# A fused patch-embedding, attention and expert block on Trainium2: query weights masked by GpSimd in five pieces, the relative rows repeated by a single DMA, a tile of value weights per batch

## The reference

```python
h = tok_ref(x, W, b, class_token, pos_embed)       # 64 images -> 65 tokens of 128 channels
h = concat([h, txt], axis=1)                        # 64 x 193 x 128
h = h + attn_ref(layernorm(h), ...)
h = h + ffn_ref(layernorm(h), ...)

def attn_ref(x, ...):                               # 8 heads, q and k of 8 channels, v of 16
    qkv = group_norm(x @ W_qkv)
    logits = einsum('bhdi,bhdj->bhij', q, k) \
           + einsum('bhdi,dij->bhij', q, rpe_k) + einsum('bhdi,dij->bhij', k, rpe_q)
    attn = softmax(logits, axis=3)
    out = einsum('bhij,bhdj->bhdi', attn, v) + einsum('bhij,dij->bhdi', attn, rpe_v)
    return group_norm(out)

def ffn_ref(x, ...):                                # 8 experts of 512, top 2 of 8, dense
    for i in range(2):
        hid = gelu(einsum('btd,edf->ebtf', x * top_p[..., i:i+1], W1) + b1)
        out = out + einsum('ebtf,efd->btd', hid, W2) + b2_sum
```

## Time and profile before

| what | value |
|---|---|
| median of 3 runs | 3904.54 us (3902.61 to 3911.96) |
| profiled execution | 3891.26 us, span 3889.4 us |
| mean granted TensorE clock | 0.952 |
| busy: PE, DVE, ACT, POOL | 85%, 56%, 50%, 31% of the span |

### The profile page before, as it was taken

The page is one execution under the profiler, slowest core; times in us unless marked ns, Lnnn a source line. Parts: engine busy times, 40 slices in busy tenths (PEclk is TensorE's granted clock), DMA queues, the critical chain, the costliest instruction groups (busy, mean ns, idle before and its releaser), DMA issues.

```text
span 3889.4 us, 66829 instructions
## 1 busy us (share of the span) xinstructions
PE 3295.7 (85%) x22496; PEld 2686.9 (69%) x22496; DVE 2164.7 (56%) x4181; ACT 1953.9 (50%) x3603; POOL 1197.8 (31%) x1191
## 2 busy tenths in 40 slices
PE   4775788988888888988888889888888889888888
PEld 4664666777677666777776667776776667777776
DVE  6883455555555555555555555555555555555554
ACT  6882344544445544544455444444455445444455
POOL 0000133332333333333233333323333333323335
PEclk9997799999999999999999999999999999999999
DMA  8771111001111111001111111011111110011110
GB/s 187 153 144 49 23 25 24 12 16 22 24 22 24 24 24 24 7 19 24 24 22 24 24 24 20 9 22 24 22 24 24 24 24 9 19 22 24 22 22 5
DMA packets 263695, 124.72 MB, mean 32 GB/s; under 512 B 118494, under 2 KB 262174, under 8 KB 263326
## 3 DMA queue, kind: packets, MB, share of 16 engines
q1 hardware_dynamic: 261250, 118.87, 15.6%
q10 hardware_dynamic: 2416, 5.47, 0.4%
HBM read 106.03 MB, written 14.97 MB: 31 GB/s over the span
## 4 chain that ended last, share of the span: by engine, by line
issue 56%; POOL 21%; PE 10%; DVE 2%; SPq 1%; ACT 1%; POOLq 1%; DMA 0%; ACTq 0%; DVEq 0%
POOL gelu L914 20%; PE bank L432 3%; PE bank L508 1%; PE bank L473 1%; PE bank L461 1%; POOL gst L927 1%; PE bank L467 1%; SPq L392 1%; PE bank L441 1%; ACT gelu L842 1%; POOLq L913 0%; PE bank L445 0%; PE bank L442 0%; DVE gelu L623 0%; PE bank L531 0%
## 5 line engine op out<-in xcount | busy, mean ns | idle before, releaser
L914 POOL TENSOR_TENSOR gelu<-gelu 128x386 f32<-128x386 f32 x1024 | 1041.1, 1025 | 2105.8 <-ACT gelu L842 2102.2
L841 ACT ACTIVATE gelu<-bank,b_s 128x386 f32<-128x386 f32 x1024 | 595.4, 581 | 1080.9 <-DVE gelu L623 1068.5
L432 PE MATMUL bank<-gelu,w_s 128*128 128x386 f32 x2048 | 855.3, 504 | 33.6 <-POOL gelu L914 30.1
L623 DVE TENSOR_TENSOR gelu<-bank,ratio 128x386 f32<-128x386 f32 x1024 | 562.9, 555 | 475.5 <-PE bank L445 469.9
L441 PE MATMUL bank<-x_hi,w_hi 128*128 128x386 f32 x1024 | 542.9, 530 | 265.9 <-ACT gelu L841 264.6
L842 ACT ACTIVATE gelu<-gelu,b_s 128x386 f32<-128x386 f32 x1024 | 623.8, 609 | 0.0
L441 PEld LDWEIGHTS bank<-x_hi,w_hi 128*128 128x128 f32 x1024 | 196.5, 192 | 441.8 <-ACT gelu L841 353.4
L531 PE MATMUL bank<-k_f,q_bd 128*128 128x193 f32 x1600 | 405.2, 336 | 58.3 <-DVE a_bd L721 58.3
L432 PEld LDWEIGHTS bank<-gelu,w_s 128*128 128x128 f32 x2048 | 374.4, 194 | 82.3 <-POOL gelu L914 57.4
L881 ACT ACTIVATE lp<-bank,mx 128x193 f32<-128x193 f32 x800 | 292.2, 419 | 253.3 <-DVE mx L731 253.3
L731 DVE TENSOR_REDUCE mx<-bank 128x2 f32<-128x386 f32 (+1 forms) x416 | 226.4, 544 | 339.0 <-PE bank L532 336.0
(11 more groups left out here) (145 smaller groups left out, 4942.3 us busy)
## 6 DMA issues: line engine op xcount, KB each, us to landing
a_rep<-u_scratch SPq DMA_DIRECT2D x256, 200.0 KB, 4.7
xt<-in_x SPq DMA_DIRECT2D x192, 196.0 KB
q_bd<-q_f SPq DMA_DIRECT2D x512, 6.2 KB
txt_s<-in_txt SPq DMA_DIRECT2D x32, 128.0 KB, 2.1
u_scratch<-k_f SPq DMA_DIRECT2D x32, 100.0 KB, 2.2
u_scratch<-q_f SPq DMA_DIRECT2D x32, 100.0 KB, 2.2
out<-o_s SPq DMA_DIRECT2D x64, 48.5 KB
out<-o_s SPq DMA_DIRECT2D x64, 48.0 KB
```

What stands on the lines that cost most here:

```text
L432: mm(yb[:, 0:T2], w2_s[:, f, :], gelu1[:, f % RING, :], start=(f == 0), stop=(f == NF - 1)).then_inc(S["w2_done"], 1)
L623: v.tensor_tensor(gelu2[:, f % RING, :], zb[f % 2][:, 0:T2], ratio[:, :], ALU.mult).then_inc(S["z2_done"], 1)
L841: a(gelu1[:, f % RING, :], zb[f % 2][:, 0:T2], ACT.Gelu, bias=b1_s[:, f:f + 1]).then_inc(S["g_done"], 1)
L914: g.tensor_tensor(gelu1[:, f % RING, :], gelu1[:, f % RING, :], gelu2[:, f % RING, :], ALU.add).then_inc(S["hs_done"], 1)
```

## The change

It does three things. POOL now makes `q_bd`: five `tensor_tensor` multiplications of 128x640, `qs0` to `qs4`, of `q_f` (repeated over bh) by a new constant mask `mask_bh` (repeated over the columns); the 16 DMAs and the clearing of `q_bd` at the start are gone. `u_scratch` is laid out as (source, d, bh, column), so that a row of 3200 numbers is what a partition of `a_rep` needs, and a single DMA reads it back with each row repeated for eight partitions. There are two tiles `v_pad0` and `v_pad1`, and `vt1` moves to a place right behind `vt0`, ahead of the logits.

```diff
-EARLY = "txt mean1 var1 inv1 bc1 proj gmean gvar gaff".split()
+EARLY = "txt mean1 var1 inv1 bc1 proj gmean gvar gaff qs0 qs1 qs2".split()
-    "c c c c am0 c am1 c am2 c am3 vt0 hkeep log0 log1 ...
+    "c qs3 c qs4 c c am0 c am1 c am2 c am3 vt0 vt1 hkeep log0 log1 ...
-    "c pv0 c vt1 rec0 pv1 c rec1 place0 ...
+    "c pv0 c rec0 pv1 c rec1 place0 ...
-    ... w2t xin w2t w2t ot a otr a ocopy hres a"
+    ... w2t xin w2t w2t ot a otr qs0 a ocopy qs1 hres a qs2"
...
+QS = (0, 5, 10, 15, 20, OCT)
-        v_pad = sb("v_pad", [P, 2, H, 32])
+        v_pad = [sb(f"v_pad{b}", [P, 2, H, 32]) for b in range(2)]
...
                 for src, x in enumerate((k_f, q_f)):
-                    sp.dma_start(u_scratch[:, src, :, :], x[:, :]).then_inc(S["u_out"], 16)
-                for bh in range(BH):
-                    rows = slice(DK * bh, DK * bh + DK)
-                    sp.dma_start(q_bd[rows, :, bh, :], q_f[rows, :].rearrange("p (o r) -> p o r", r=8)).then_inc(S["q_spread"], 16)
+                    sp.dma_start(u_scratch[src, :, :, :].rearrange("d b i -> b d i"), x[:, :]).then_inc(S["u_out"], 16)
                 sp.wait_ge(S["u_out"], t * 32 + 32)
-                for r in range(8):
-                    sp.dma_start(a_rep[r:P - 7 + r:8, :, :], u_scratch[:, :, :, :].rearrange("b s d i -> (s d) b i")).then_inc(S["a_spread"], 16)
+                sp.dma_start(a_rep[:, :, :], u_scratch[:, :, :, :].rearrange("s d b i -> (s d) (b i)").unsqueeze(1)
+                             .broadcast_to([2 * DK, 8, BH * LP])).then_inc(S["a_spread"], 16)
...
             def copy_v(b, t):
                 act.wait_ge(S["vt"], t * 2 + b + 1)
-                if b == 1:
-                    act.wait_ge(S["pv_done"], t * 2 + 1)
+                if not is_first(t):
+                    act.wait_ge(S["pv_done"], t * 2 - 1 + b)
...
+                elif s[:2] == "qs":
+                    o0, o1 = QS[int(s[2]):int(s[2]) + 2]
+                    if s == "qs0":
+                        pool.wait_ge(S["norm"], t * 4 + 2)
+                        if not is_first(t):
+                            pool.wait_ge(S["log_ready"], t * FILLS)
+                    g.tensor_tensor(q_bd[:, o0:o1, :, :],
+                                    q_f[:, 8 * o0:8 * o1].rearrange("p (o r) -> p o r", r=8).unsqueeze(2).broadcast_to([P, o1 - o0, BH, 8]),
+                                    K["mask_bh"].unsqueeze(1).unsqueeze(3).broadcast_to([P, o1 - o0, BH, 8]), ALU.mult).then_inc(S["q_spread"], 1)
...
-            g.memset(q_bd[:, :, :, :], 0.0).then_inc(S["setup_pool"], 1)
```

More of the change, by code:

```diff
@@ L72 @@
 _at = 0
-for _n, _w in (("ident", P), ("ones", P), ("g8", P), ("g4", P), ("mask_r", 8), ("mask_q", 8), ("place", HD + HD + HD)):
+for _n, _w in (("ident", P), ("ones", P), ("g8", P), ("g4", P), ("mask_bh", BH), ("mask_r", 8), ("mask_q", 8), ("place", HD + HD + HD)):
     CO[_n] = (_at, _w)
@@ L96 @@
 FILLS = (OCT + 1) // 2
-N_QS, N_AS = 16 * BH, 16 * 8
+QS = (0, 5, 10, 15, 20, OCT)
 LOGS = 4
@@ L408, in _ @@
                 sp.wait_ge(S["h_ready"], t * 2 + 2)
-                tokens(t + 1, lambda: sp.wait_ge(S["log_ready"], t * FILLS) if t else sp.wait_ge(S["setup_pool"], 1))
+                tokens(t + 1, lambda: sp.wait_ge(S["log_ready"], t * FILLS) if t else None)
                 spread(t)
@@ L523, in attend @@
                     if i == 0:
-                        pe.wait_ge(S["q_spread"], t * N_QS + N_QS)
+                        pe.wait_ge(S["q_spread"], t * (len(QS) - 1) + len(QS) - 1)
                         pe.wait_ge(S["a_masked"], t * 4 + 4)
@@ L558, in attend @@
                                     hh = 2 * j + e
-                                    w = v_pad[0:jn, c, hh, :] if z == 0 else one_pad[0:jn, e, :]
+                                    w = v_pad[b][0:jn, c, hh, :] if z == 0 else one_pad[0:jn, e, :]
                                     m = mm(pv[b][32 * j:32 * j + 32, 256 * z:256 * z + LP], w,
@@ L719, in attend @@
                     if s == "am0":
-                        dve.wait_ge(S["a_spread"], t * N_AS + N_AS)
+                        dve.wait_ge(S["a_spread"], t * 16 + 16)
                     v.tensor_tensor(a_bd[:, o0:o1, :, :],
@@ L808, in _ @@
             v.memset(half[:, 1:2], 2.718281828459045).then_inc(z, 1)
-            v.memset(v_pad[:, :, :, :], 0.0).then_inc(z, 1)
+            v.memset(v_pad[0][:, :, :, :], 0.0); v.memset(v_pad[1][:, :, :, :], 0.0).then_inc(z, 1)
             dve.wait_ge(z, 5)
@@ L845, in copy_v @@
                 act.wait_ge(S["vt"], t * 2 + b + 1)
-                if b == 1:
-                    act.wait_ge(S["pv_done"], t * 2 + 1)
+                if not is_first(t):
+                    act.wait_ge(S["pv_done"], t * 2 - 1 + b)
                 for c, (j0, jn) in enumerate(JC):
-                    blk = v_pad[0:jn, c, :, :].rearrange("p h n -> p (h n)")
+                    blk = v_pad[b][0:jn, c, :, :].rearrange("p h n -> p (h n)")
                     dst = bass.AP(tensor=blk.tensor, offset=blk.offset, ap=[list(blk.ap[0]), [64, H // 2], [32 + HD, 2], [1, HD]])
@@ L948, in build @@
     tok_scratch = nc.dram_tensor("tok_scratch", (P, B, NPATCH), F32, kind="Internal").ap()
-    u_scratch = nc.dram_tensor("u_scratch", (BH, 2, DK, LP), F32, kind="Internal").ap()
+    u_scratch = nc.dram_tensor("u_scratch", (2, DK, BH, LP), F32, kind="Internal").ap()
     with ExitStack() as ctx:
@@ L968, in shape_constants @@
     put("g4", (p[:, None] // 4 == p[None] // 4) / 4.0)
+    put("mask_bh", p[:, None] // DK == np.arange(BH)[None])
     put("mask_r", p[:, None] // HD == np.arange(8)[None])
```

## The result

The changed kernel takes 3681.1 us (median; 3674.57 to 3684.06), the kernel before 3903.57 in the same comparison. The ratio is 0.9428 (95% interval 0.9403 to 0.9453): 5.7% faster, some 223 us. The prediction had the direction but said 3789, and its range ended at 3715, above the result. The profiled execution has a span of 3682.3 us.

The account below looks back on a forecast made before the run. Bound: DVE idles 6.75 us before am0 for a_rep, whose reads queue behind 16 DMAs. 31 x (1.7 + 1.7) = 105 us plus 11 in the first turn: 3891 - 116 = 3775 profiled, 3789 us median; range 3715 to 3880.

Parts of the forecast that it names:

- Part 3: Second transposes ahead of the logits: 1.70 us of PE between pv0 and pv1 go; new wait for ACT's copies before the first logit.
- The gain of the stage is 1.7 us a turn: Masking stage up to the first logit: it comes at 2109.2 instead of 2110.87, 1.7 us earlier each turn.
- walk: Forecast schedule of one turn: POOL's pieces at 1.66 us and sums, then DVE's masks alternating with sums, to the first logit.
- The end of sum 3: POOL's line of pieces and sums: sum 3 ends at 2100.9, with pieces at 1.66 us.
- The end of `am3`: DVE's last mask, alternating with POOL's sums for the port: ends at 2108.9, or 2106.9 without the exclusion.
- The first logit: PE's first logit, 1.9 us behind chunk 9 after ACT's copies and transposes: taken at 2109.2, where it was 2110.87.
- cost nothing that I can see: Slow matmuls at clock 0.55 in the 6.41 us behind the stall: no cost, since DVE is busy 6.26 us of it.
- 116: Total gain in us: 31 x (1.7 + 1.7) = 105, plus 11 in the first turn.
- `pv1`: PE between pv0 and pv1: the two transposes and the wait for copies go, 1.7 us a turn.
- Cheap pieces: Rival: POOL's pieces cost 1.0 us each, sum 3 ends at 2098.4, 5.9 us gained a turn, 3724 median; chance 0.12.
- POOL wins the port: Rival: am0 gets in only when POOL runs dry after sum 6, 0.7 us left a turn, 3872; chance 0.10.
- Dear pieces: Rival: POOL's pieces cost 3.3 us, 85 us slower, 3989; gains used up at 2.7 us a piece; chance 0.15.

Follow-up runs that it names:

- e6: Kernel before with one edit: SP issues the eight reads of a_rep ahead of the 16 DMAs into q_bd; 3660 us, 0.9329 of before.
- e3: Changed kernel, but a_rep read back by eight DMAs from the old scratch layout; 0.9422 of before.
- e1: Kernel before with only the two tiles of value weights and the second transposes ahead of the logits; 3873 us, 0.9897 of before.
- e7: Kernel before with a single a_rep read ahead of the 16 q_bd DMAs and two value-weight tiles, no masks on POOL; 0.9237 of before.
- e8: As e7, but the second transposes stand behind the last logit instead of ahead of the first; 0.9228 of before.
- e2: Changed kernel without the two value-weight tiles and the moved second transposes; 0.9509 of before.
- e11: e8 with POOL's sums of chunks 3 to 9 cut to 8 of 386 columns; 0.9130 of before.
- e12: e8 with DVE's masks one chunk earlier, the first behind chunk 5, chunk 9 after the last; 0.9121 of before.
- e13: Changed kernel with POOL's pieces 3 to 5 behind sum 7, masks one chunk earlier, second transposes behind the last logit; 3565.5 us, 0.9106 of before.
- e5: Changed kernel with each of POOL's five pieces made twice behind the first turn, once into a spare tile; 0.9818 of before.

## Why the prediction was wrong, point by point

**What bounds the kernel.** Right. The stall in front of `am0` was the queue's order (e6), the DMA is hidden by more than 5 us (issued at 2075.70, landed 9.8 later, first mask at 2091.12), and the form of the reads does not matter (e3).

**The sizes.** Part 3 was right: 1.2 us a turn net, measured 40 and 32 us. The step that failed is the term "The gain of the stage is 1.7 us a turn": the direction and the order of the steps were right, the size was not. It measured 4.15. Shift the times of the changed kernel by 7.93 us, so that they can be laid beside the forecast's walk from step to step, and it compares like this.

The end of sum 3: forecast 2100.9, measured about 99.2 (2090.23 + 1.0 + 7.93). Three pieces at 1.3 to 1.4 instead of 1.66 are 1.0 us of that; the other 0.7 are waits that I had let DVE's `x_lo` and `hres` impose: `x_lo` took 0.67 instead of 0.56 us, and sum 0 came where it had been (2083.47 + 7.93 = 2091.40).

The end of `am3`: forecast 2108.9, measured 98.22 + 7.93 = 2106.15, so another 1.0 us within the masking stage. It has as many sums and masks as I had given it, but a sum and a short mask together take less: `am2` ends 1.69 us behind `am1`, and `am3` 1.68 behind `am2`, where the walk had 2.9 (with two sums) and 2.0; between `am0` and `am1`, where the trace has the two sums, it is 2.65 and the walk had 2.0 with one. From the end of `am0` that is 6.0 us instead of 6.9.

The first logit: forecast 2109.2, measured 2106.7. So 2.5 us of 31 turns, 76 us, were lost in the walk.

**The clock.** The prediction said that the slow matmuls behind the stall "cost nothing that I can see". In the turn that I had looked at that is so. In six of the 31 turns behind the first the granted clock was still at its lower level when the logits began. One such turn of the kernel before, on PE:

```profile
1446.17 0.98 PE L531 MATMUL bank<-k_f,q_bd 128*128 128x193 f32 x2 [1.13 <-DVE a_bd L721]
1446.95 0.85 PE L532 MATMUL bank<-rw,a_bd 128*128 128x193 f32 x2
...
1450.81 0.84 PE L532 MATMUL bank<-rw,a_bd 128*128 128x193 f32 x2
1451.45 0.53 PE L531 MATMUL bank<-k_f,q_bd 128*128 128x193 f32 x2
```

Windows of the first logits, that turn and the one of the prediction:

```profile
core 0: us, PE busy (x) PEld busy (x) DVE busy (x) ACT busy (x) POOL busy (x), PEclk, DMA share, GB/s
1446.10:1452.00 5.90, 5.83 (x20) 5.86 (x21) 0.87 (x2) 2.60 (x6) 0.92 (x1) 0.54 0.00 0
2110.87:2116.00 5.13, 5.13 (x31) 5.13 (x32) 1.68 (x3) 3.60 (x9) 0.85 (x1) 1.00 0.00 0
```

From 1446.17 to 1451.45 there are eight groups of two in 5.3 us; the second window has 31 matmuls in 5.13 us, a group of two each 0.33 us, half as long. Such turns are 111.7 to 112.2 us long in place of 109. Over the 30 turns the gain is 6.2 us each (185.5 / 30), where the turn that I compared shows 5.75; that makes 13 us.

Not all of it is this clock. The changed kernel has such turns too, five of them, 105.0 to 105.6 us long in place of 103.3, with a granted clock of 0.71 to 0.73 over the first 5.9 us of the logits, though DVE does not wait for a DMA there. Six turns with some 2.6 us too much against five with some 2.2 leave about 5 us for the clock. Another 4 to 5 are in the stall: DVE waited 234.4 us in 32 waits, 20.15 of them in the first turn, so 6.91 us in the mean of the others, and the turn that I had picked had 6.75. The rest, some 3 us, stays open.

The sum with what was measured: 116 + 76 for the walk, less 3 for `pv1` (1.6 instead of 1.7), + 13 + 4 at the end of the first phase = 206; the spans say 207. As the 13 are themselves taken from the turns' lengths, the sum shows that no large term is missing, not that each is understood. I read one turn where I should have read the spread of them.

The low clock at the first logits comes and goes from kernel to kernel: in the profiles it is in 19 turns of e1 (granted 0.71 to 0.79 there), 14 of e7, 13 of e8 (102.5 to 103.1 us long beside 100.8), one of e6, and none of e2, e11, e12 and e13. What brings it on was not found. A difference of 10 to 20 us between two of these kernels can be this alone, and part of what e11 and e12 win over e8 is.

**The rivals.** None of them came as it was put. "Cheap pieces" was nearest, with 5.9 us a turn, for a piece of 1.0 us; the turn won 5.8 at 1.3, so its price was wrong as well, by the same walk. "POOL wins the port" did not happen in that form. "Dear pieces" put the break-even at 2.7 us; e5 with 2.6 us a piece was still 1.8% faster than before, so the break-even lies above that. The range failed because every one of its cases went through the same walk, so that an error in it moved them all one way; it was also added up wrongly: 31 x 5.9 + 11 is 194 us, which from 3891 gives 3697 in the profile and 3710 as a median, not 3711 and 3724, so that even the cheap pieces lay just outside the 3715 that was meant to take them in. And the bounds of the walk's other steps (the waits for the port, the turn that was picked) were not in it.

**The signs named.** DVE's idle time, the landing (9.8), the group x160, the number of waits for sums and the clock in the masking stage (1.00) came as said; the pieces took 1.29 us in the median and 1.39 in the mean, not 1.6 to 1.8, and the waits of PE for sums were at most 0.8 us rather than 1.5. Neither of the two things named as making the prediction wrong, pieces over 2.7 us and a landing past 2100, came about.

## What to carry to other kernels

When a DMA lands late, read the queue that issued it before making the transfer faster: here sixteen issues of 0.74 us that nobody needed yet stood ahead, and exchanging two loops gave more than moving the work to another engine. Work moved to an idle engine costs by what stands behind it in that engine's queue: three of the five masks cost 75 us between the sums and nothing that could be told where the sums behind them were needed only after the logits. When a step of a hand-made schedule is freed, look at once for the next one in the list (the masks one chunk earlier gave another 1.1%), and read the length of every turn, not of one, before putting a number on a stall.

## What the runs showed of the hardware

- GpSimd's multiplication with both inputs repeated took 1.28 us and more (median 1.29, mean 1.39) for 128x640 and 0.43 for 128x128, against 1.00 us for a plain sum of 128x386.
- A mask on VectorE with two inputs in SBUF fell from 1286 to 953 ns when GpSimd's sums beside it were cut to 8 columns.
- One DMA of 1600 KB, 12.8 KB rows each repeated for eight partitions, lands in 9.5 to 10.0 us. In the first turn, where the mask waits for the data, it starts 9.9 us behind the issue of the one DMA and 10.8 behind the first of the eight in e3.
- Behind a stall in which TensorE did nothing for some 6.7 to 6.9 us, the granted clock was back at its higher level 6.4 us behind the start of the first mask in one turn of the kernel before (logits from 2110.87) and still at the lower one 11 us behind it in another (1439.76 to 1450.81).
- In the changed kernel the clock fell with no such stall: in one turn it was 1.00 from the first mask to the first logit (948.47 to 956.14), with PE busy 5.48 of 7.67 us, and 0.50 over the first logits (956.14 to 958.00), with PE busy throughout.
